# Cross-attention and mixture of experts: the routed rows' clear in pieces, the last head normalised in the next stage, results added straight into the output, and token scatters in groups of four

## The reference

```python
x = x + attention(ctx, layernorm(x), mask, ...)     # softmax(q k) v @ Wout + bout
x = x + moe(layernorm(x), ...)
# moe: shared = gelu(xf @ Wfc_s + bfc_s) @ Wproj_s + bproj_s
#      the 2 largest of softmax(xf @ Wr) per token, renormalised: the gates
#      for each of 8 experts: h = gelu(xf @ Wfc[e] + bfc[e]) @ Wproj[e] + bproj[e]
#      routed += h * gate[:, e]
#      shared + routed
```

## Time and profile before

| what | value |
|---|---|
| median of 3 runs | 2884.76 us (2877.29 to 2886.98) |
| the profiled execution | 2891.44 us, span 2889.9 |
| PE busy | 2540.3 us, 88%, 14668 matmuls |
| DVE, ACT, POOL busy | 65%, 59%, 45% |
| granted TensorE clock | 0.946 of full speed |
| DMA | 480.51 MB, mean 166 GB/s |

### The profile page before, as it was taken

How to read it: one execution, slowest core, us unless ns; L and a number is a source line. 1 busy time by engine, 2 the same in 40 slices (tenths; PEclk the granted TensorE clock), 3 DMA queues, 4 the chain that set the end, 5 groups by cost and what they waited for, 6 DMA issues and landing times. The chain is left out here.

```text
span 2889.9 us, 45231 instructions
## 1 busy us (share of the span) xinstructions
PE 2540.3 (88%) x14668; PEld 2073.3 (72%) x14668; DVE 1869.1 (65%) x2423; ACT 1702.8 (59%) x2296; POOL 1289.6 (45%) x766
## 2 busy tenths in 40 slices
PE   2475999999999999999999999859865999999993
PEld 1354777777777777777777777639865999999993
DVE  6143677777777776777777776638732556666665
ACT  2154777777777777877877877733311344444441
POOL 1431554544544544534535535415353026556552
PEclk7697999999999999999999999979876999999996
DMA  5569456456555555464564564447331069999996
GB/s 193 145 188 157 118 159 162 129 153 155 145 146 150 142 152 143 142 161 134 144 167 126 154 167 119 124 109 170 95 112 55 1 206 304 305 299 299 305 305 211
DMA packets 273327, 480.51 MB, mean 166 GB/s; under 512 B 76007, under 2 KB 157083, under 8 KB 268648
## 3 DMA queue, kind: packets, MB, share of 16 engines
q1 hardware_dynamic: 232600, 416.87, 51.6%
q0 software_dynamic: 15280, 47.76, 4.9%
q10 hardware_dynamic: 25376, 14.99, 2.8%
HBM read 295.16 MB, written 79.51 MB: 130 GB/s over the span
## 5 line engine op out<-in xcount | busy, mean ns | idle before, releaser
L658 DVE TENSOR_TENSOR pr_lo<-pr,pr_hi 128x1024 fp32r<-128x1024 f32 x576 | 820.1, 1432 | 422.8 <-ACT pr_hi L737 418.3
L736 ACT ACTIVATE pr<-ps_s 128x1024 f32<-128x1024 f32 x512 | 526.6, 1028 | 324.8 <-PE ps_s L808 314.1
L737 ACT ACTIVATE pr_hi<-ps_s 128x1024 fp32r<-128x1024 f32 x512 | 522.3, 1020 | 0.0
L822 PE MATMUL ps_o<-pr_hi,vA 128*65 128x512 f32 x1152 | 465.6, 404 | 20.2 <-DVE o_sb L599 11.0
L824 PE MATMUL ps_o<-pr_lo,vA 128*65 128x512 f32 x1152 | 455.7, 396 | 0.0
L823 PE MATMUL ps_o<-pr_hi,vC 128*65 128x512 f32 x1152 | 454.1, 394 | 0.0
L503 POOL TENSOR_TENSOR sq<-raw 128x1024 f32<-128x1024 f32 (+1 forms) x96 | 182.9, 1905 | 607.2 <-ACT raw L712 607.2
L808 PE MATMUL ps_s<-qq_hi,kk 128*128 128x512 f32 x1152 | 362.9, 396 | 45.3 <-ACT pr_hi L737 38.7
L1424 ACT ACTIVATE ht<-f_ps_h,b 128x256 f32<-128x256 f32 x448 | 188.0, 471 | 364.4 <-PE f_ps_h L1356 279.9
L1356 PE MATMUL f_ps_h<-xT_hi,w 128*128 128x256 f32 x1792 | 365.9, 288 | 19.2 <-issue 15.8
L505 POOL TENSOR_TENSOR rs<-ss,minus_half 128x16 f32<-128x16 f32 (+1 forms) x96 | 258.7, 2695 | 265.5 <-DVE ss L645 265.5
(11 more groups left out here) (178 smaller groups left out, 3896.3 us busy)
## 6 DMA issues: line engine op xcount, KB each, us to landing
w<-w1S_dram SPq DMA_DIRECT2D x164, 512.0 KB, 8.0
lnT_sb<-lnT_dram SPq DMA_DIRECT2D x32, 2304.0 KB, 8.6
w2raw<-in_L_ffn_Wproj SPq DMA_DIRECT2D x80, 512.0 KB, 7.9
qq_hi<-q_hi SPq DMA_DIRECT2D x128, 256.0 KB, 4.8
qq_lo<-q_lo SPq DMA_DIRECT2D x128, 256.0 KB, 5.0
kk<-k_hi SPq DMA_DIRECT2D x64, 288.0 KB, 5.2
kk<-k_lo SPq DMA_DIRECT2D x64, 288.0 KB, 5.3
w1S_dram<-cut POOLq DMA_DIRECT2D x36, 512.0 KB, 4.1
```

What stands on the lines that cost most here:

```text
L658: v.tensor_tensor(pr_lo[:, d % RING, :], pr[:, d % 2, :], pr_hi[:, d % RING, :].bitcast(F32), ALU.subtract).then_inc(s_lo, 1)
L736: act.activation(pr[:, d % 2, :], ps_s[:, d % 2, :], ACT.Exp, bias=bias)
L737: act.activation(pr_hi[:, d % RING, :], ps_s[:, d % 2, :], ACT.Exp, bias=bias).then_inc(s_exp, 1)
L822: mm(out, upper, pr_hi[:, r, cols], start=k == 0, stop=False)
```

## The change

Four things are joined.

1. *The clear*. `routed` has 10752 rows of 258 elements. POOL clears them in 28 DMAs, one a window in windows 2 to 29, from a tile `empty` that holds zeros and, as a float in column 256, the number of a spare row. Those spare rows (256) now stand behind the output.
2. *The last head*. Its numerators stay in o_second, which outlives attention. ACT, DVE and SP do its denominators, division and store in `project_out`, beside the first quarters of sample 0; SP waits for the store before the last sample. wo comes after the first a and in halves.
3. *Expert results*. Shared tile m's x2 is written to the output at once by SP. A row of `routed` carries its token's number and gate as floats. DVE multiplies y by the gate, and POOL's scatter adds to the token's row of the output (`compute_op`), waiting each time until the previous tile's has landed. There are 39 routed tiles, x is loaded four tiles ahead, and `combine` is gone. The function returns the first 4096 rows of the output.
4. *The scatters of tokens* go in groups of four (TOGETHER); POOL waits for all earlier ones to land before each further group.

```diff
-ROUTED += ROUTED % 2
-ROWS = (ROUTED + 1) * TS
-WIDE = D + 1
+ROWS = (ROUTED + 3) * TS
+WIDE = D + 2
+SPARE = TS
+TOGETHER = 4
+CLEARED = ROWS // TS // (WINDOWS // 2 - 2)
...
+            def clear(w):
+
+                rows = routed[bass.ds(w.v * (CLEARED * TS) - CLEARED * TS, CLEARED * TS), :]
+                pool.dma_start(rows.rearrange("(j r p) d -> r p j d", r=2, p=P)[w.s],
+                               empty[:, w.s, :].unsqueeze(1).broadcast_to([P, CLEARED, WIDE])).then_inc(s_clear, 16)
...
+                if not isinstance(w.v, int):
+                    clear(w)
...
-                    if w.first and d == UNITS - 1:
-                        act.dma_start(routed[:, 0:D].rearrange("(t p) d -> p t d", p=P),
-                                      zero[:, :].unsqueeze(1).broadcast_to([P, ROWS // P, D])).then_inc(s_clear, 16)
-                        act.dma_start(routed[:, D:WIDE].rearrange("(t p) d -> p t d", p=P),
-                                      spare[:, :].bitcast(F32).unsqueeze(2), allow_slow_non_contiguous=True).then_inc(s_clear, 16)
...
-            sp.dma_start(wo[:, :, :], Wout.rearrange("(k p) n -> p k n", p=P)).then_inc(s_w, 16)
-
             def batch(b):
+                if b == B - 1:
+                    sp.wait_ge(s_store, 16)
...
+                    if b == 0 and q == 0:
+                        for h in range(2):
+                            sp.dma_start(wo[:, HH * h:HH * h + HH, :], Wout.rearrange("(h k p) n -> h p k n", h=2, p=P)[h]).then_inc(s_w[h], 16)
...
+                    if b == 0 and q == G - 1:
+                        sp.wait_ge(s_norm, 1)
+                        sp.dma_start(attT[HEADS - 1], o_second[0:DH, :]).then_inc(s_store, 16)
...
+            last = rden[HEADS - 1:HEADS, :]
+            act.dma_start(last, o_second[DH:DH + 1, :]).then_inc(s_put, 16)
+            act.dma_start(den[:, :], last.rearrange("h (p k) -> p (h k)", p=P)).then_inc(s_den, 16)
+            act.wait_ge(s_inv, 1)
+            act.dma_start(last.rearrange("h (p k) -> p (h k)", p=P), den[:, :]).then_inc(s_put, 16)
...
+                        act.wait_ge(s_put, 32)
+                        act.dma_start(rec, last.broadcast_to([DH, N])).then_inc(s_rec, 16)
...
+                    if b == 0 and q == 0:
+                        dve.wait_ge(s_rec, 16)
+                        v.tensor_tensor(o_second[0:DH, :], o_second[0:DH, :], rec, ALU.mult).then_inc(s_norm, 1)
...
-                if shared and m + 2 >= SHARED:
-                    if s == 0:
-                        sp.wait_ge(s_sc, 16 * 2 * TT)
-                    load_x(routed_v, m + 2 - SHARED, s)
-                elif not shared and left >= 2:
-                    sp.wait_ge(s_xt, m + 1)
-                    sp.sem_inc(s_go, 1)
-                    sp.wait_ge(s_home, m - (SHARED - 1))
-                    load_x(routed_v, m + (2 - SHARED), s)
+                if shared and m + 2 == SHARED:
+                    sp.wait_ge(s_sc, 16 * 2 * TT)
+                    for k in range(2):
+                        load_x(routed_v, k, k)
...
+                if left >= 5 and (not shared or m + 2 >= SHARED):
+                    sp.wait_ge(s_ahead, m - (SHARED - 3))
+                    load_x(routed_v, m + (4 - SHARED), s)
...
+                if shared:
+                    sp.wait_ge(s_sum, m + 1)
+                    sp.dma_start(base_v[m], x2[:, 2 * m:2 * m + 2, :]).then_inc(s_base, 16)
...
-                pool.iota(l2[:, :, D:WIDE].bitcast(I32), pattern=[[2 * P, TT], [0, 1]], base=k, channel_multiplier=2).then_inc(s_num, 1)
-                pool.wait_ge(s_num, k + 1)
+                nc.gpsimd.tensor_copy(l2[:, :, D + 1:WIDE], gates[:, :, k:k + 1]).then_inc(s_num, 1)
+                pool.wait_ge(s_num, k + 2)
                 for tile in range(TT):
+                    if tile % TOGETHER == 0 and tile:
+                        pool.wait_ge(s_sc, 16 * (k * TT + tile))
                     pool.indirect_dma_start(out=routed[:, :], out_offset=bass.IndirectOffsetOnAxis(ap=slots[:, k, tile:tile + 1], axis=0),
                                             in_=l2[:, tile, :], in_offset=None).then_inc(s_sc, 16)
...
-                pool.wait_ge(s_yv, U * 2 + (s + 1))
+                if isinstance(U, int) and U == S2 and s == 0:
+                    pool.wait_ge(s_base, 16 * SHARED)
+                else:
+                    pool.wait_ge(s_ys[1 - s], (U - (S2 - s)) * 32)
+                pool.wait_ge(s_yw, U * 4 + (2 * s + 2 - 2 * SHARED))
                 pool.wait_ge(s_home, U * 2 + (s + 1 - SHARED))
                 pool.sem_inc(s_go, 1)
                 for r in range(2):
-                    pool.indirect_dma_start(out=ys[:, :], out_offset=bass.IndirectOffsetOnAxis(ap=home[:, s, r:r + 1], axis=0),
-                                            in_=y[:, s, r, :], in_offset=None).then_inc(s_ys[s], 16)
-
-            def pair(U, first=False, last=False):
+                    pool.indirect_dma_start(out=out[:, :], out_offset=bass.IndirectOffsetOnAxis(ap=home[:, s, r:r + 1], axis=0),
+                                            in_=y[:, s, r, :], in_offset=None, compute_op=ALU.add).then_inc(s_ys[s], 16)
...
+                    if p == 1 and not shared:
+                        if not (isinstance(U, int) and U == S2):
+                            dve.wait_ge(s_ys[s], (U - S2) * 32)
+                        dve.wait_ge(s_ahead, m - (SHARED - 1))
+                        v.tensor_copy(weight[:, s, :], ahead[:, s, :, 1])
+                        v.tensor_copy(home[:, s, :], ahead[:, s, :, 0]).then_inc(s_home, 1)
...
+                            v.tensor_copy(ahead[:, s, :, :], xt[:, s, :, D:WIDE]).then_inc(s_ahead, 1)
...
-                    v.tensor_copy(home[:, 1 - s, :], xt[:, 1 - s, :, D].bitcast(I32)).then_inc(s_home, 1)
...
+                else:
+                    dve.wait_ge(s_yv, m + 1)
+                    for r in range(2):
+                        v.tensor_scalar(y[:, s, r, :], y[:, s, r, :], weight[:, s, r:r + 1], None, ALU.mult).then_inc(s_yw, 1)
...
-def combine(nc, x2, gates, ys, out):
...
-                    for tile in range(2):
-                        n = 2 * k + tile
-                        nc.vector.scalar_tensor_tensor(x2[:, n, :], y[:, i, tile, j, :], gates[:, n, j:j + 1], x2[:, n, :],
-                                                       ALU.mult, ALU.add).then_inc(done, 1)
```

More of the change, by code:

```diff
@@ L290, in windows, with attention @@
         body(Window(WINDOWS // 2 - 1, s))
-def attention(nc, qn_g, kn_g, lnT, Wq, Wkv, maskRow, maskCol, attT, rden, routed, Wfc_s, Wfc, w1S):
+def attention(nc, qn_g, kn_g, lnT, Wq, Wkv, maskRow, maskCol, attT, rden, routed, out, Wfc_s, Wfc, w1S, o_second):
     with ExitStack() as ctx:
@@ L863, in __init__, with project_out @@
         self.s_b1, self.s_b2 = ([t.sem("f_%s_%d" % (n, i)) for i in range(2)] for n in ("b1", "b2"))
-def project_out(nc, x, Wout, bout, Wr, attT, l2, x2, logit, early, weights_s, w1S):
+def project_out(nc, x, Wout, bout, Wr, attT, rden, o_second, l2, x2, logit, early, weights_s, w1S):
     HP, G = H // 2, 4
@@ L1100, in _, with experts @@
             logits(B - 1, G - 1)
-def experts(nc, early, weights_s, weights, w1S, logit, gates, expert, slots, l2, routed, x2, ys):
+def experts(nc, early, weights_s, weights, w1S, logit, gates, expert, slots, l2, routed, x2, out, o_second):
     b1_s, Wproj_s, b2_s = weights_s
@@ L1326, in _ @@
                 pair(u)
-            pair(LAST, last=True)
-            scatter(LAST, 1)
+            scatter(LAST - 1, 1)
+            scatter(LAST, 0)
         @block.tensor
```

159 lines of the change are left out of this document (72 added, 87 removed).

## The result

The changed kernel takes 2678.59 us (median of 4, 2676.51 to 2682.29), the kernel before 2884.08 beside it: a ratio of 0.929, with an interval of 0.927 to 0.931. That is 205.5 us less; I had said 118 less (2766), and my range, 2685 to 2808, begins above what was measured.

What follows compares the result with a forecast made beforehand. TensorE holds the clock nearly everywhere, with DMA close behind in routed tiles and four stretches almost without PE work. Terms -50 - 17 - 36 - 21 + 5 = -119 gave 2772 us, 2766 at the median's scale; range 2685 to 2808.

Steps and rivals of the forecast that it cites:

- The clear: 200 to 280 us: ACT loses its issues and waits, POOL issues 28 hidden transfers instead; -50 us, bounds -40 and -53.
- the 700 that I had written: In the clear: the 28 transfers' 11 MB spread over some 700 us at DMA share 0.54.
- The last head: 1901 to 1935 us: earlier barrier, loads start 14.3 us sooner, a ahead of halved Wout; -17 us, bounds -12 and -19.
- a arrives later than that, so it is hidden: Last head: DVE's reciprocal waits 4.56 us ahead of rounding a, at no cost; if a hung on it, -12.
- The end: After the last y: two scalings, two scatters and their landing replace loads, multiply-adds and stores; 12 us left, -36.
- The routed tiles: 39 tiles of 12.4 us instead of 40 of 12.62; -21 us, bounds -43 and -13.
- The DMA engines set the floor: Routed tiles: DMA busy 11.9 us a tile; if adding doubles q0's 0.65 us, the floor is 12.5 us.
- never fit without a hole: Routed tiles: 12.4 us taken, above the middle of 11.83 to 12.6, since two resources are both nearly full.
- The scatters of tokens: 2126 to 2209 us: groups of four take 107 us instead of 85, pauses give back 13 us; net +5, bounds -15 and +20.
- What does a pause give PE? ... so 7 more for one pause: Scatters of tokens: the one existing pause shows 7 more matmuls, 0.9 us of work; 14 new pauses give back 13 us.
- the 71 us that I had left in the sum: Scatters of tokens: 101 matmuls in 83 us are 12.0 us of work, so 71 us are lost.
- My rival A: Scatters of tokens: the pauses lift the stall, 71 us less with about 5 left, total 2696; chance 33%.

Runs made afterwards that it cites:

- The experiment with home moved: Kernel before, last column copied aside when x is split, home made from it mid-step instead of in front of y: 2851.2 us against 2877.9 (0.991).
- groups of 16: Changed kernel with the scatters of tokens in groups of 16 instead of four, with their waits: 2746.5 us.
- The series in a loop: Changed kernel with added work: POOL issues 16 scatters into a buffer of their own once a turn in its loop of routed tiles: 2970.8 us.
- the series of 32: Changed kernel with all 32 scatters of a choice in one series again (TOGETHER 32): 2753.5 us, 0.956 of before.

## Why the prediction was right or wrong

**The clear** (-50, measured -52.4): right in mechanism and size, as far as the trace shows; no run took this part by itself. In the stretch where ACT had stood 39.91 us PE has its 377 matmuls, with the first of the 28 pieces in it. The pieces spread over 1446 us, 262 to 1708, twice the 700 that I had written, and each takes POOL 0.84 us.

**The last head** (-17, measured -14.4): the mechanism was right, and terms were mis-sized. The loads started 3.7 us after the last value product, where I had 2.8 (1.7 us of it for the barrier, which no row gave). I took 4.56 us for the inversion's wait from the trace before and wrote that "a arrives later than that, so it is hidden". The wait was 12.24 us, and a's rounding hung on it. Yet taking the rounding out from behind it moved it by less than a microsecond, since a itself lands late. And I left out what follows the rounding of a: Wout's rounding and low part now stand behind it, 5.7 us to the first product against 4.7 before. The 16 groups behind it took 124.9 us instead of 120.8, which I had put at nothing and haven't taken apart.

**The end** (-36, measured -35.1): right in size, in part by luck. The terms that I listed add up to 7.6 to 12.2 us, not to the 8.6 to 13 that I wrote, with 2 us for the last semaphores that no row gave. I had the wait for the scatter before as covered by the same landing; it cost 3.08 us in front of the last scatter. The whole took 13.1 us, against the 12 that I had taken.

**The routed tiles** (-21, measured -39): the direction was right and the term too small. The step that failed is "The DMA engines set the floor". I multiplied the time of a tile by a busy share of 0.94 and called the product a bound, and went above the middle because two nearly full resources "never fit without a hole". It is no bound, and they do fit: PE runs at full pace with the share at 1.04 (q0 at 14.0%) and at 0.98 (overwriting) alike, and the kernel before reaches the same 11.83 us with a share of 0.95 once home is moved. What cost 0.8 us a tile was a chain of waits through DVE and SP, of which I saw the piece home's copy to y and not where it ended. The experiment with home moved gave 27 us (2877.9 - 2851.2); with the tile that is no more, at 11.8, that is the 39 measured.

**The scatters of tokens** (+5, measured -75): here the prediction failed. The step is "What does a pause give PE? ... so 7 more for one pause". I read the effect of a pause from a stretch in which the stall had been there for 30 us, and laid it onto pauses that come before it has set in. The runs show that these are different things: two more pauses of 1.8 us inside a stall gave 7 us of 75 (groups of 16), and with 1.2 us of other work behind each four scatters the stall never comes. What decides is the mean spacing: 1.28 us a scatter in one series stalls PE, the change's 1.86 doesn't, and the 71 us that I had left in the sum are gone. My rival A had the clue, "as if something filled up and drained", and 33%. Its price was short too: it left 5 us of stall and kept the routed tiles at my wrong floor. The Trainium skill ("Runtime: NRT & Kernel Launch", Instruction fetch mechanics) says that each sequencer fetches its instructions over a DMA queue of its own; from that I had thought of fetches held up by descriptors. The series in a loop doesn't bear that out: PE is held up there with no instruction packet in 500 us.

The Trainium skill ("Collectives: The Full Stack", Stop 4, SDMA + CCE) says of collectives that the add comes free with the two reads and the write. For the kernel's time that holds here too: 2677.0 us without the add, 2678.6 with it. For the DMA engines it isn't nothing: q0's share is 5.5% without and 14.0% with it, 2.5 times, in three times the packets (960 and 2880 in 120 us), where I had estimated one and a half times by the page and doubled it in my sum.

What stays open is which part of the chip is filled by scatters issued faster than one in about 1.5 to 1.6 us. The runs exclude the rows and bytes of a scatter and the landing. The DMA engines' share was 0.24 to 0.28 in the stalls of the tokens' scatters and 0.36 to 0.40 without one, and a fetch isn't needed. What fits all runs is something that each scatter uses once, that drains at a rate of its own, and without which PE and ACT can't go on; that is argued, not shown.

## What to carry to other kernels

A long, dense series of indirect DMAs on POOL held up TensorE and ScalarE here, with 64 rows as with 128; it shows as idle time on PE with "issue" as its reason, some eight to ten scatters after the first, and spacing the scatters (a third of a microsecond of other work behind each, or groups of four with a wait) removed all of it here. A busy share of the DMA engines near 1 is no floor: look for the wait by name, and follow it through the queue that is issued in order behind it (here DVE's y, then SP's loads). And an effect read inside a saturated stretch says nothing on what the same thing does before saturation.

## What the hardware showed that I had not expected

- Scatters of 128 rows of 1032 bytes, one in 1.28 us, leave PE 0.6 matmuls a microsecond of 8.5; one in 1.62 us leaves it all. In between it depends steeply on the spacing (6.2 at 1.46).
- The stall sets in 10 to 14 us after the first scatter of a dense series (one in 1.20 to 1.34 us), for 64 rows as for 128; at one in 1.46 us after some 23; in the loop of routed tiles, behind other scatters, after 6.
- PE went nearly idle first and its clock fell after that: the last 72 us of the series of 32 have it at 0.50, 1.2 GHz.
- Adding scatters have three times the packets of plain ones and 2.5 times their share of the DMA engines (5.5% to 14.0%) at the same bytes.
